# Attention's products as float16 pairs, split on GpSimd, in a graph network kernel

## The reference

```
z  = einsum('ni,hif->nhf', h, W)          # 1250 nodes, 4 heads, 256 features
el = einsum('nhf,hf->nh', z, a_l);  er = einsum('nhf,hf->nh', z, a_r)
e  = leaky_relu(el[src] + er[dst], 0.2)   # 20000 edges
m  = segment_max(e, dst)
ex = exp(e - m[dst]);  s = segment_sum(ex, dst)
out = segment_sum((ex / s[dst])[:, :, None] * z[src], dst)
```

## Time and profile before

| | us |
|---|---|
| median of 3 runs | 2622.9 |
| lowest, highest | 2618.68, 2627.12 |
| the profiled execution | 2623.34 |
| its span, first to last instruction | 2620.7 |
| the first block of attention in it | 270.3 to 332.1 |
| the second block | 332.6 to 512.0 |

### The profile page before, as it was taken

The page is one execution under the profiler, slowest core; times in us unless marked ns, Lnnn a source line. Parts: engine busy times, 40 slices in busy tenths (PEclk is TensorE's granted clock), DMA queues, the critical chain, the costliest instruction groups (busy, mean ns, idle before and its releaser), DMA issues. The chain is left out here.

```text
span 2620.7 us, 34756 instructions
## 1 busy us (share of the span) xinstructions
PE 2476.7 (95%) x12681; PEld 1671.7 (64%) x12681; DVE 1968.6 (75%) x2499; ACT 1220.8 (47%) x1402; POOL 144.3 (6%) x172
## 2 busy tenths in 40 slices
PE   6999289889999999999999999999999899999898
PEld 4666178756666666666666666666666566577665
DVE  7876889788888897797798788788878655755222
ACT  5322566565545455545545545555543245521111
POOL 1000000010000000000000000000000010000122
PEclk9999699979999999999999999999999999999999
DMA  5211410143232322422422322223241046653993
GB/s 162 63 37 39 86 59 1 51 139 77 72 62 56 78 57 56 94 56 40 95 55 47 88 71 59 60 72 62 56 117 35 16 160 209 226 186 130 359 355 104
DMA packets 145398, 252.01 MB, mean 96 GB/s; under 512 B 67144, under 2 KB 82122, under 8 KB 138854
## 3 DMA queue, kind: packets, MB, share of 16 engines
q1 hardware_dynamic: 135394, 231.41, 31.2%
q0 software_dynamic: 4928, 10.25, 1.6%
q10 hardware_dynamic: 4932, 8.30, 0.9%
HBM read 204.01 MB, written 49.34 MB: 97 GB/s over the span
## 5 line engine op out<-in xcount | busy, mean ns | idle before, releaser
L1683 PE MATMUL wide_ps<-keep_own_w1g,rails_hid_hi 128*125 128x512 f16 x2120 | 632.5, 380 | 2.9 <-DVE rails_hid_lo L1400 2.9
L1683 PE MATMUL wide_ps<-keep_own_w,rails_hid_hi 128*125 128x512 f16 x2080 | 618.9, 379 | 1.4 <-issue 1.4
L1683 PE MATMUL wide_ps<-keep_own_w1g,rails_hid_lo 128*125 128x512 f16 x1060 | 402.7, 380 | 0.0
L1683 PE MATMUL wide_ps<-keep_own_w,rails_hid_lo 128*125 128x512 f16 x1040 | 394.2, 379 | 0.0
L1683 PEld LDWEIGHTS wide_ps<-keep_own_w1g,rails_hid_hi 128*125 128x125 f16 x2120 | 285.6, 137 | 157.7 <-issue 4.5
L1683 PEld LDWEIGHTS wide_ps<-keep_own_w,rails_hid_hi 128*125 128x125 f16 x2080 | 279.3, 136 | 154.2 <-DVE keep_X L1454 3.6
L1175 ACT ACTIVATE rails_hid_hi<-rails_raw_a,keep_scale_hidden 128x1000 f16<-128x1000 f32 x210 | 274.7, 1334 | 208.9 <-DVE rails_raw_a L1428 94.2
L1165 ACT ACTIVATE rails_raw_a<-wide_ps,keep_scale_gelu 128x1000 f32<-128x1000 f32 (+1 forms) x192 | 182.1, 952 | 332.9 <-PE wide_ps L1668 329.8
L1400 DVE SCALAR_TENSOR_TENSOR rails_hid_lo<-rails_raw_a,keep_scale_hidden,rails_hid_hi 128x1000 f16<-128x1000 f32 x210 | 312.0, 1515 | 32.7 <-ACT rails_hid_hi L1175 32.5
L1454 DVE SCALAR_TENSOR_TENSOR keep_X<-wide_ps,rails_out_scale,keep_X 125x1024 f32<-125x1024 f32 x180 | 198.5, 1103 | 140.8 <-PE wide_ps L1683 140.8
L909 PE MATMUL wide_ps<-att_zh,counts_room 125*125 125x257 f32 x800 | 175.6, 382 | 31.5 <-DVE counts_room L807 31.5
(11 more groups left out here) (463 smaller groups left out, 3784.5 us busy)
## 6 DMA issues: line engine op xcount, KB each, us to landing
carried_w_land<-cproj SPq DMA_DIRECT2D x79, 1024.0 KB
ffn_w_up<-split_d SPq DMA_DIRECT2D x11, 2048.0 KB, 12.9
keep_X<-split_d SPq DMA_DIRECT2D x6, 2048.0 KB, 10.8
ffn_w<-W SPq DMA_DIRECT2D x11, 1024.0 KB, 8.0
rails_xs<-xt_d SPq DMA_DIRECT2D x124, 78.1 KB
keep_comb_hi<-W SPq DMA_DIRECT2D x8, 1024.0 KB, 7.3
split_d<-graph_high SPq DMA_DIRECT2D x16, 512.0 KB, 6.7
keep_own_w1g<-W SPq DMA_DIRECT2D x6, 1024.0 KB, 6.0
```

Source lines behind the costliest of these rows:

```text
L1683: mm = nc.tensor.matmul(ps[0:P, t, :], hid[(q + b) % 2][l][:, k, t * P:(t + 1) * P], w[(q + b) % 2][r][:, k, :], start=(k == 0 and i == 0) ...
```

## The change

GpSimd makes float16 pairs of both operands of attention's products, and TensorE multiplies the pairs.

In the first block z is no longer loaded into its place. It lands by half heads (125 x 5 x 256) in two buffers, `land`, which lie in `row_b`. GpSimd scales each piece by `z_up`, a power of two from `w_two`, copies it to the high part in float16 and subtracts that from the piece to get the low part: three instructions for each of eight pieces, each waiting for the one before. SyncE loads piece i when piece i - 2 has been split. `w_two` moves to memory that is kept beyond the opening, and VectorE makes `z_up` with one small operation.

In the second block weigh writes float32 weights into two buffers, and waits until GpSimd has made the low part of two steps earlier. GpSimd, idle there before, copies the weights of each step to a high part and subtracts to get the low part, into three rooms for pairs. TensorE waits for the low part and makes three float16 products where there was one float32 product. The take multiplies the sum of the weights by `z_up`.

```diff
@@ attention, first block
-                for h in range(HEADS):
-                    rows_to(sp, zh[:, h, :, 0:HEAD_F], z_d.rearrange("(t p) (h f) -> p h t f", p=P, h=HEADS)[:, h], z_in[h])
+                z_rows = z_d.rearrange("(t p) (h f) -> p h t f", p=P, h=HEADS)
+                for i in range(2 * HEADS):
+                    if i >= LANDS:
+                        sp.wait_ge(z_lo_set, i - LANDS + 1)
+                    rows_to(sp, land[i % LANDS], z_rows[:, i // 2, (i % 2) * HALF_T:(i % 2 + 1) * HALF_T, :], z_in[i % LANDS])
 
             @block.gpsimd
             def _(pool):
-                nc.gpsimd.memset(zh[:, :, :, HEAD_F:ZW], 1.0).then_inc(ones_set, 1)
+                nc.gpsimd.memset(z_of["hi"][:, :, :, HEAD_F:ZW], 1.0)
+                nc.gpsimd.memset(z_of["lo"][:, :, :, HEAD_F:ZW], 0.0).then_inc(ones_set, 1)
+                pool.wait_ge(z_up_set, 1)
+                for i in range(2 * HEADS):
+                    part = (slice(None), i // 2, slice((i % 2) * HALF_T, (i % 2 + 1) * HALF_T), slice(0, HEAD_F))
+                    pool.wait_ge(z_in[i % LANDS], 32 * (i // LANDS + 1))
+                    nc.gpsimd.tensor_scalar(land[i % LANDS], land[i % LANDS], z_up[:, 0:1].bitcast(F32), None, ALU.mult).then_inc(z_hi_set, 1)
+                    pool.wait_ge(z_hi_set, 2 * i + 1)
+                    nc.gpsimd.tensor_copy(z_of["hi"][part], land[i % LANDS]).then_inc(z_hi_set, 1)
+                    pool.wait_ge(z_hi_set, 2 * i + 2)
+                    nc.gpsimd.tensor_tensor(z_of["lo"][part], land[i % LANDS], z_of["hi"][part], ALU.subtract).then_inc(z_lo_set, 1)
...
+                nc.vector.tensor_scalar(z_up[:], w_two[0:P, :], -1.0, float(INVERT + (Z_TOP << 23)), ALU.mult, ALU.add).then_inc(z_up_set, 1)
@@ attention, second block
+            @block.gpsimd
+            def _(pool):
+                for m in range(STEPS):
+                    part = wt_of[m % PAIR_ROOMS]
+                    pool.wait_ge(wt_set, m + 1)
+                    if m >= PAIR_ROOMS:
+                        pool.wait_ge(used, m - PAIR_ROOMS + 1)
+                    nc.gpsimd.tensor_copy(part["hi"], wt[m % 2]).then_inc(wt_hi_set, 1)
+                    pool.wait_ge(wt_hi_set, m + 1)
+                    nc.gpsimd.tensor_tensor(part["lo"], wt[m % 2], part["hi"], ALU.subtract).then_inc(wt_lo_set, 1)
...
                 def weigh(m):
                     h, half, s = body[m]
-                    if m >= DEEP:
-                        dve.wait_ge(used, m - DEEP + 1)
+                    if m >= 2:
+                        dve.wait_ge(wt_lo_set, m - 1)
                     dve.wait_ge(exp_set, m + 1)
-                    nc.vector.scalar_tensor_tensor(wt[m % DEEP], wexp[m % 2], 1.0,
+                    nc.vector.scalar_tensor_tensor(wt[m % 2], wexp[m % 2], 1.0,
                                                    ct[:, s, half * HALF:(half + 1) * HALF], ALU.min, ALU.mult).then_inc(wt_set, 1)
...
-                        ins = nc.vector.tensor_scalar(total[:, b:b + w], ps_o[:, b:b + w, HEAD_F], 1e-30, None, ALU.max)
+                        ins = nc.vector.tensor_scalar(total[:, b:b + w], ps_o[:, b:b + w, HEAD_F], 0.5, z_up[:, 0:1].bitcast(F32),
+                                                      ALU.max, ALU.mult)
...
-                        pe.wait_ge(z_in[h], 32)
+                        pe.wait_ge(z_lo_set, 2 * h + 2)
...
-                    pe.wait_ge(wt_set, m + 1)
+                    pe.wait_ge(wt_lo_set, m + 1)
...
-                        mm = nc.tensor.matmul(ps_o[:, bank(g, d), 0:ZW], wt[m % DEEP][:, d * P:(d + 1) * P],
-                                              zh[:, h, s, :], start=(s == 0), stop=(s == TILES - 1))
+                        for n, (l, r) in enumerate(SPLIT):
+                            mm = nc.tensor.matmul(ps_o[:, bank(g, d), 0:ZW], wt_of[m % PAIR_ROOMS][l][:, d * P:(d + 1) * P],
+                                                  z_of[r][:, h, s, 0:ZW], start=(s == 0 and n == 0), stop=(s == TILES - 1 and n == 2))
```

More of the change, by code:

```diff
@@ L96, in rows_to, with opening @@
     queue.dma_start(to[WIDE:P], source[WIDE:P]).then_inc(done, 16)
-def opening(nc, ident, room, counts, ct, cnt, deg, indeg, X_all, x, w, a_l, a_r, z_d, el, er, src, dst, maker, up, combs, scales, spare, eps):
+def opening(nc, ident, room, counts, ct, cnt, deg, indeg, X_all, x, w, a_l, a_r, z_d, el, er, src, dst, maker, up, combs, scales, spare, eps, w_two):
     OCTETS = RAILS // 8
@@ L645, in attention @@
     ZW = HEAD_F + 1
-    DEEP = 4
+    LANDS = 2
+    PAIR_ROOMS = 3
+    Z_TOP = 4
     TAKE_LAG = 3
@@ L651, in attention @@
         row_a, row_b = c.sb("row_a", [P, HEADS, NODES], F32), c.sb("row_b", [P, HEADS, NODES], F32)
-        zh = c.sb("zh", [P, HEADS, TILES, ZW], F32)
+        z_of = {n: c.sb(f"z_{n}", [P, HEADS, TILES, ZW + 1], F16) for n in ("hi", "lo")}
+        land = [row_b[:, 1:HEADS, :].rearrange("p h d -> p (h d)")[:, k * HALF_T * HEAD_F:(k + 1) * HALF_T * HEAD_F]
+                .rearrange("p (t f) -> p t f", f=HEAD_F) for k in range(LANDS)]
+        z_up, pair_room = c.sb("z_up", [P, 1], I32), c.sb("pair_room", [P, HALF], F32)
+        z_up_set, z_hi_set, z_lo_set = c.sem("z_up_set"), c.sem("z_hi_set"), c.sem("z_lo_set")
         max_el, top, peak = [c.sb(n, [P, TILES, HEADS], F32) for n in ("max_el", "top", "peak")]
@@ L662, in attention @@
         far = c.sb("far", [P, 1], F32)
-        z_in = [c.sem(f"z_in{k}") for k in range(HEADS)]
+        z_in = [c.sem(f"z_in{k}") for k in range(LANDS)]
         edgeless, maxed, cols_set = c.sem("edgeless"), c.sem("maxed"), c.sem("cols_set")
@@ L762, in attention @@
         cells = cnt[:].rearrange("p t d -> p (t d)").bitcast(F32)
-        pieces = [cells[:, k * HALF:(k + 1) * HALF] for k in range(6 + DEEP)]
-        low, arg, wexp, wt = pieces[0:2], pieces[2:4], pieces[4:6], pieces[6:6 + DEEP]
+        pieces = [cells[:, k * HALF:(k + 1) * HALF] for k in range(8 + PAIR_ROOMS - 1)] + [pair_room[:]]
+        low, arg, wexp, wt = pieces[0:2], pieces[2:4], pieces[4:6], pieces[6:8]
+        wt_of = [{n: room.bitcast(F16)[:, i * HALF:(i + 1) * HALF] for i, n in enumerate(("hi", "lo"))} for room in pieces[8:]]
+        wt_hi_set, wt_lo_set = c.sem("wt_hi_set"), c.sem("wt_lo_set")
         low_set, arg_set, exp_set, wt_set = c.sem("low_set"), c.sem("arg_set"), c.sem("exp_set"), c.sem("wt_set")
@@ L2809, in program @@
         deg, indeg = keep.sb("deg", [P, TILES], F32), keep.sb("indeg", [P, TILES], F32)
+        w_two = keep.sb("w_two", [128, 1], I32)
         std, eps = keep.sb("std", [P, TILES], F32), keep.sb("eps", [P, 1], F32)
@@ L2830, in program @@
             ct, cnt = [room[0:P, k * TILES * NODES:(k + 1) * TILES * NODES].rearrange("p (t d) -> p t d", t=TILES) for k in range(2)]
-            opening(nc, ident, room, counts, ct, cnt, deg, indeg, X_all, x, W0, a_l, a_r, z_d, el, er, src, dst, maker, up, combs, scales, spare, eps)
+            opening(nc, ident, room, counts, ct, cnt, deg, indeg, X_all, x, W0, a_l, a_r, z_d, el, er, src, dst, maker, up, combs, scales, spare, eps, w_two)
             wide = ctx.enter_context(ExitStack())
             ps = Core(nc, wide, "wide").ps("ps", [128, 8, BANK])
-            attention(nc, X, ident, ct, cnt, z_d, el, er, deg, dis, stat_parts, spare, mean_var, std, rstd, rstd_up, eps, ps, rows_d)
+            attention(nc, X, ident, ct, cnt, z_d, el, er, deg, dis, stat_parts, spare, mean_var, std, rstd, rstd_up, eps, ps, rows_d, w_two)
         recycle(nc)
```

4 lines of the change are left out of this document (2 added, 2 removed).

## The result

The changed kernel takes 2753.0 us, the median of four runs (2749.18 to 2761.59), against 2624.6 us before, also of four (2618.68 to 2627.12). The ratio is 1.048, with a 95% interval of 1.047 to 1.050: 128 us more. The forecast was 2785 us, thus 161 us more.

The account below looks back on a forecast made before the run. VectorE was taken to bound the first block, TensorE the second. With VectorE and GpSimd excluding each other, 2623 us + 121 (second block) + 40 (first block) = 2784, say 2785 us; range 2695 to 2875.

Parts of the forecast that it names:

- the step of 3.4 to 3.9 us: Second block: a sign of being right, TensorE's idle time ending on the subtraction, with a step of this length.
- What bounds the kernel, and what the pairs give TensorE: VectorE sets the first block, TensorE the second; fifteen float16 products cost 1.67 us a step against 2.19.
- the forecast's cheap rival: Second block: no exclusion, subtraction at 0.62 us, VectorE the bound at 152 us against 179; 2596 us, chance 0.05.
- Exclusion, and both ways: Both blocks: VectorE operations with two SBUF inputs and GpSimd operations reading SBUF each wait for the other; +121 and +40 us.
- one-way waiting: Both blocks: rival, GpSimd waits for VectorE, VectorE never waits; step 3.1 us, total 2702 us, chance 0.13.
- no exclusion: Both blocks: rival, engines never exclude each other, subtraction at 1.24 us; second block 176 us, total 2620, chance 0.07.
- The second block's step, 3.65 us: Second block: 0.78 + 0.72 + 0.62 + 1.24 us plus 0.3 for hand-overs, 292 us for 80 steps.
- The 0.3 us for hand-overs: Second block: time per step for passing turns between VectorE and GpSimd, bounds 0 and 0.6 us.
- The first block, 42.7 us of GpSimd: First block: 24 GpSimd instructions, 40.3 us plus waits, exclude the maxima; block ends at 372 instead of 332, +40 us.
- z's loads hidden, the take-outs at 0.5 us each: First block: z's loads land while GpSimd splits; second block: seven take-outs add 0.5 us each, 3.5 us.
- TensorE's clock: Second block: products take 1.67 us a step, or 3.3 at the lower clock, beneath the 3.65 us step either way.
- the last one's 2915 us: Both blocks: rival, GpSimd much slower than its cast, with exclusion; subtraction 2.5 us, step 4.9, chance 0.09.

Follow-up runs that it names:

- the last kernel: Against the kernel with z split by ScalarE and VectorE and weights' high part by ScalarE: third weights buffer taken from low, tiny early subtraction; 2687.3 us, ratio 1.024.

## Why the prediction was right, and where its size was off

The direction and the mechanism held, and the time lies inside the range, though 32 us below the 2785 forecast; of the signs listed for being right, the step of 3.4 to 3.9 us didn't come. By its steps:

**What bounds the kernel, and what the pairs give TensorE**: right. At the upper clock the products are 0.11 us apart as priced (393.89 and 394.00); with GpSimd out of the way the second block falls to 154.4 us, against 152 for VectorE's bound in the forecast's cheap rival.

**Exclusion, and both ways**: right, and the step that decided. VectorE's side of it, which no row of before showed, is seen in L832 at 1565 and L840 at 1362 ns, and shown by the pair of kernels with PSUM and SBUF constants (181.3 against 260.5 us). The Trainium skill, "SBUF — State Buffer", section "Who interferes with whom", names just these conditions: two SBUF inputs on VectorE, and on GpSimd an instruction that reads and doesn't only write. The trace agrees with each of them (858 and 805 ns with PSUM inputs, 865 and 810 beside fills). It doesn't agree that the lock is held for the whole instruction, as the forecast had taken over from that section: of VectorE's 0.72 and 0.78 us from start to start 0.65 to 0.67 stood in GpSimd's way. Of the rivals, one-way waiting falls with this; no exclusion would have given 181.3 for the second block, close to the 176 worked out for it.

**The second block's step, 3.65 us**: this is the term that was mis-sized; measured 3.03 to 3.14, 3.1 in the mean. The copy and the subtraction were well priced: 0.70 and 1.3 alone against 0.62 and 1.24, and 0.6 and 1.2 of them exclusive. Two other parts were too large. The 0.3 us for hand-overs is about zero: the records overlap, and it seems that the next instruction, already issued, has its start-up behind it when the one before ends. By the same reading VectorE's two operations count with 0.65 us each in the chain and not with their 0.78 and 0.72 from start to start. 0.3 + 0.2 us, and 0.05 for GpSimd's two, times 80, are 44 us; 3 for the statistics and 1.5 for the ends go the other way, and that turns +121 into the +80 that was measured. The 0.21 us behind VectorE's end, on which the hand-over rested, lay within the all-reduce's own 0.35, as the forecast itself remarks; that they were its work and not a hand-over is the likely reading.

**The first block, 42.7 us of GpSimd**: right in kind (+40 forecast, +46 measured), wrong in its parts, whose errors cancel in part. The scaling was priced like a copy, at 1.26; it takes 3.5 us alone and 2.7 from VectorE. The copy takes 1.0 and the subtraction 2.3 of the 1.26 and 2.52 assumed, and the waits cost nothing. 2.7 + 1.0 + 2.3 times eight are 48, less the 1.8 of pauses. So the nearness of 40 and 46 is in part luck. The remark that starving GpSimd until the maxima end would come to the same was wrong: the kernel that split z behind the maxima was 10 us slower.

**z's loads hidden, the take-outs at 0.5 us each**: right; no wait on z shows in the first block, and steps with a take-out are 0.4 to 0.5 us longer. The statistics, put wholly beneath GpSimd, add 0.2 us each, 3 in all. **TensorE's clock**: the forecast let it lie beneath at either level, since it had 3.3 us for a step at the lower one against 3.65. Against the real step of 3.1 that no longer holds; the clock stood at it for the first 13 us of the block and fell to it six times later, for no more than 6.8 us each, and no wait of GpSimd or VectorE came of it.

**The rivals' prices**: the last one's 2915 us doesn't follow from its own terms, which give about 2906 (1.26 us more a step in the second block, 21 more in the first); nothing hangs on it.

Summed, the step's error is -40, the first block's +6, and the rest of the program took 5 us more where nothing was forecast: 161 - 40 + 6 + 5 = 132, and the profiled span grew by 131.

Left open: the 5 us of the rest, 0.2% of it, in which nothing was changed. In the profiled executions of the experiments the rest took 2108.8 to 2115.6 us, so at least a part of the 5 is the spread from one execution to the next. And no version was found in which attention's products as pairs beat the kernel before. With both operations of VectorE and one subtraction holding each other off, 0.65 + 0.65 + 1.2 = 2.5 us a step is an estimate of the least while GpSimd subtracts (the plain steps of the last kernel had 2.5 in the mean); TensorE's float32 products took 2.19. To have the real second inputs in PSUM wasn't tried: the five sums and their overlap between groups take the banks.

## What to carry to other kernels

An engine that is idle by its busy share isn't free to use: in this kernel work on GpSimd that reads SBUF was taken out of VectorE's time wherever VectorE's instructions read two SBUF tensors, so price it as if both were one engine, by the sum of their data times and without hand-overs. Look for that waiting in durations that have grown, not in the table of waits, and settle it with a control that moves one operand to PSUM and changes no wait. And before moving work to relieve an engine, ask what the relieved engine's neighbours allow: here VectorE alone needs 154 of the 180 us, so at most 26 could be won, and the splitting cost 106.

## What the runs showed of the hardware

- Of a 125x625 float32 VectorE operation with two SBUF inputs, recorded at 0.80 to 0.86 us alone, 0.65 to 0.67 us shut GpSimd out; of GpSimd's 0.70 us copy 0.56, of its 1.3 us subtraction 1.15 to 1.25. The rest overlaps.
- With such instructions ready on both engines they took turns in the steps read above; neither was starved. Only the scaling of z with its factor in SBUF let a second maximum pass first.
- GpSimd's multiplication of 125x1280 float32 by a scalar takes 3.52 us, more than its two-input subtraction with float16 output (2.50) and 2.8 times its cast (1.25). Whether that is the float32 output or the operation wasn't separated.
- GpSimd's first subtraction stood 7.3 and 9.15 us idle before it began, its first scaling 9.34 us, and the subtraction behind that scaling nothing; attention's copies and fills had no such wait (a copy had already run in the opening). An early subtraction of two columns hid it, which was worth 5.5 us in the block.
- TensorE's clock at its lower level, for 3.4 to 6.8 us at a time in the middle of the block, cost nothing beside a step of 3.1 us: neither GpSimd nor VectorE waited for TensorE in that block.
